# One mamba-and-attention decoder layer: two silus, the output projections and the keys and values in other slots of the scan

## What is computed

```python
x = x + mamba(layernorm(x))                        # the phase that the change touches
x = x + cross_attention(ctx, layernorm(x), mask)   # 750 keys per element, 16 heads
x = x + ffn(layernorm(x))                          # 2048 hidden, binarised weights, gelu
```

```python
xz = rmsnorm(h) @ W_in;  x, z = split(xz)          # 512 -> 2 x 1024
x = silu(conv4(x) + conv_b)
x_dbl = x @ W_x                                    # -> 64 for dt, 16 for B, 16 for C
dt = softplus(x_dbl[..., :64] @ W_dt + b_dt)
h[t] = exp(dt * A) * h[t-1] + (dt * x) * B         # 1024 x 16 states, over 224 steps
y = sum_n(h * C) + x * D
out = residual + (y * silu(z)) @ W_out
```

## Time and profile before

| | us |
|---|---|
| median of three runs | 3689.96 |
| the profiled execution | 3689.67 |
| its span, first to last instruction | 3688.3 |
| mamba phase: start of the first and of the last scan | 83.7 and 1983.8 |
| windows 1 to 13 together | 1563.2 |
| windows 14 and 15 | 114.2 and 103.3 |
| PE, DVE, ACT, POOL busy over the span | 3250.6, 2664.2, 2377.3, 1773.9 |

### The profile page before, as it was taken

One profiled execution on the slowest core, in us unless ns is written; L12 is line 12 of the kernel. 1 busy time (PEld: TensorE's weight loads), 2 busy tenths in 40 slices (PEclk: granted clock), 3 DMA queues, 4 the chain that ended last, 5 costly groups with the idle time before them and its releaser, 6 DMA issues. The chain is left out here.

```text
span 3688.3 us, 59573 instructions
## 1 busy us (share of the span) xinstructions
PE 3250.6 (88%) x20864; PEld 2278.9 (62%) x20864; DVE 2664.2 (72%) x4681; ACT 2377.3 (64%) x5276; POOL 1773.9 (48%) x1052
## 2 busy tenths in 40 slices
PE   5678888988898889898996799999999999789998
PEld 4556655666566656665563566666666666467887
DVE  2999999989898999889985566776766676422221
ACT  5877788677877787778863566766666666432222
POOL 2778787778877787878783000000000000035454
PEclk8799999999999999999998899999999999889999
DMA  6646756566657665666563231211211121111010
GB/s 172 185 121 178 192 164 159 158 185 181 164 139 199 182 158 153 181 188 160 143 183 101 74 90 45 82 51 45 74 58 45 50 82 46 30 54 46 23 46 23
DMA packets 286440, 425.14 MB, mean 115 GB/s; under 512 B 28641, under 2 KB 226273, under 8 KB 281538
## 3 DMA queue, kind: packets, MB, share of 16 engines
q1 hardware_dynamic: 273920, 410.75, 40.3%
q10 hardware_dynamic: 12226, 10.59, 1.0%
HBM read 320.25 MB, written 101.02 MB: 114 GB/s over the span
## 5 line engine op out<-in xcount | busy, mean ns | idle before, releaser
L704 POOL TENSOR_TENSOR a_hs<-a_rep,a_bmat 128x896 f32<-128x896 f32 x512 | 1060.2, 2092 | 327.2 <-PE a_yps L278 326.9
L603 DVE TENSOR_TENSOR_SCAN a_states<-a_states,a_hs 128x900 f32<-128x900 f32 x384 | 780.6, 2033 | 116.1 <-ACT a_states L384 111.7
L384 ACT ACTIVATE a_states<-a_rep,a_a_neg 128x224 f32<-128x224 f32 x2048 | 795.7, 438 | 69.3 <-DVE a_hs L610 66.9
L1208 DVE CUSTOM_DVE_ANT_0 b_sc<-b_sps,b_mask 112x375 f32<-112x375 f32 x1024 | 499.9, 544 | 148.3 <-PE b_sps L1019 148.0
L1035 PEld LDWEIGHTS b_tps<-b_ident,b_sc 112*125 112x125 f32 x3072 | 402.9, 191 | 279.3 <-issue 142.4
L1301 POOL TENSOR_TENSOR b_xt<-b_xt,b_bo 112x512 f32<-112x512 f32 x32 | 40.9, 1300 | 1067.9 <-DVE b_ln L1185 1067.9
L1035 PE MATMUL b_tps<-b_ident,b_sc 112*125 112x112 f32 x3072 | 492.9, 290 | 69.4 <-ACT b_sc L1126 45.3
L1126 ACT ACTIVATE b_sc<-b_sc,b_nmax 112x750 f32<-112x750 f32 x512 | 467.7, 915 | 51.9 <-DVE b_nmax L1214 51.9
L300 PE MATMUL a_work<-a_hT,w_in 128*128 128x224 f32 x2048 | 444.1, 374 | 52.4 <-ACT a_hT L416 46.1
L300 PEld LDWEIGHTS a_work<-a_hT,w_in 128*128 128x128 f32 x2048 | 410.8, 203 | 93.1 <-ACT a_hT L416 49.8
L610 DVE TENSOR_TENSOR a_hs<-a_states,a_cmat 128x896 f32<-128x896 f32 x384 | 419.0, 1091 | 13.2
(11 more groups left out here) (143 smaller groups left out, 4925.4 us busy)
## 6 DMA issues: line engine op xcount, KB each, us to landing
a_rep<-du_scratch SPq DMA_DIRECT2D x512, 224.0 KB, 5.7
w_in<-W_in_dram SPq DMA_DIRECT2D x128, 512.0 KB, 4.2
du_scratch<-a_du SPq DMA_DIRECT2D x16, 1792.0 KB, 10.9
ctx<-ctxT_dram SPq DMA_DIRECT2D x48, 500.0 KB, 5.2
v_scratch<-kv_out SPq DMA_DIRECT2D x96, 250.0 KB
k_scratch<-kv_out SPq DMA_DIRECT2D x96, 250.0 KB, 4.0
b_keys<-k_scratch SPq DMA_DIRECT2D x16, 1500.0 KB, 11.7
b_v<-v_scratch SPq DMA_DIRECT2D x16, 1500.0 KB
```

The source lines that it names most:

```text
L384: e = act.activation(rows(states[:, g % DA, :])[:, q, 1:ROW], rep[tile % REPS][:, j, 0, :], ACT.Exp, scale=a_neg[:, g % SLOTS, q:q + 1])
L603: dve.tensor_tensor_scan(state if g % G4 else whole, state, whole, 0.0, ALU.mult, ALU.add).then_inc(S["scan"], 1)
L704: pool.tensor_tensor(hs[g % RING][:, :, 1:ROW], rep[tile % REPS][:, j, 1, :].unsqueeze(1).broadcast_to([P, Q, L]), bmat[b % 2][:], ALU.mul ...
L1208: dve.tensor_tensor_reduce(out=sc[block % 2][:, j, cols], in0=sps[0:TT, j, 0:HALF], in1=mask[:, block % 2, cols], scale=-1.0, scalar=3.0e3 ...
```

## The change

Three edits to the tables, one to a condition. Both halves of the output projection move two slots later (11 and 14 become 13 and 16), and with them the residuals and the store of x1; the statistics of x1 stay in slot 20. In `LATER` the row statistics go from slot 3 to 4, the logs one slot earlier (9, 11, 13, 15), silu_z from 19 to 20. Silu_x stays. Of the keys and values units of a window the one in 13 goes to 11, that in 16 to 15, that in 20 to 18, and the one in 3 of the next window to 1 (in the element before the last, 13 to 11 and 16 to 15). The order of values and keys stays the same.

```diff
--- before.py
+++ after.py
@@ -125,7 +125,7 @@
     CHUNKS = t["ctxT"].shape[2] // KC
     WIDE = 2 * KC
     BEHIND = 4
-    O_SLOTS = (39 + BEHIND, 42 + BEHIND)
+    O_SLOTS = (41 + BEHIND, 44 + BEHIND)
     UNITS = 2 * CHUNKS
     OUTS = len(shared.kv_out)
     assert TT <= P and 2 * L <= BANK and R + 2 * N <= P and CHUNK <= 2 * BANK and R == 64 and DG == 32
@@ -212,12 +212,12 @@
             "series": spaced(14, 1), "logs": spaced(15, 1), "skip": [18, 19], "spread": [17], "dt_sum": [20],
             "silu_z": [21], "u": [21], "store_du": [22]}
         LATER = {
-            "load": [-68], "row_stats": [-65], "squares": [-60], "guess": [-58], "gains": [-54], "h": [-53], "hT": [-51],
+            "load": [-68], "row_stats": [-64], "squares": [-60], "guess": [-58], "gains": [-54], "h": [-53], "hT": [-51],
             "keep_hT": [-50], "load_x": spaced(-52, 4), "load_z": spaced(-50, 4), "x": spaced(-49, 4), "tap": spaced(-48, 4),
             "older_taps": spaced(-47, 4), "z": spaced(-47, 4), "keep_z": spaced(-46, 4), "residual": [-35], "silu_x": [-33],
             "x_dbl": [-32], "xd": [-31], "store_bc": [-31], "dt": spaced(-30, 2), "parts": spaced(-29, 2),
-            "series": spaced(-28, 2), "logs": spaced(-26, 2), "skip": [-20, -19], "spread": [-19], "dt_sum": [-18],
-            "silu_z": [-17], "u": [-16], "store_du": [-15]}
+            "series": spaced(-28, 2), "logs": spaced(-27, 2), "skip": [-20, -19], "spread": [-19], "dt_sum": [-18],
+            "silu_z": [-16], "u": [-16], "store_du": [-15]}
         when = [FIRST, SECOND] + [{name: [b * SLOTS + BEHIND + at for at in slots_of] for name, slots_of in LATER.items()}
                                   for b in range(2, B)]
 
@@ -225,8 +225,8 @@
 
             return [(b, i) for b in range(B) for i, at in enumerate(when[b].get(name, ())) if at == slot]
 
-        usual = (1, 3, 5, 9, 12, 16, 18, 20, 22, 24, 26, 31)
-        last_but_one = (1, 3, 5, 9, 12, 14, 15, 16, 18, 19, 20, 22, 23, 24, 26, 27, 28, 30)
+        usual = (1, 3, 5, 7, 11, 14, 18, 20, 22, 24, 26, 29)
+        last_but_one = (1, 3, 5, 7, 11, 14, 15, 16, 18, 19, 20, 22, 23, 24, 26, 27, 28, 30)
         last = (-1, 1, 2, 3, 5, 6, 8, 9, 12, 13, 14, 16, 17, 18, 20, 21, 22, 24)
         kv_slot = ([w * SLOTS + BEHIND + at for w in range(1, B - 2) for at in usual]
                    + [(B - 2) * SLOTS + BEHIND + at for at in last_but_one] + [(B - 1) * SLOTS + BEHIND + at for at in last])
@@ -665,7 +665,7 @@
                     at = slot - b * SLOTS
                     if at - 2 in O_SLOTS:
                         add_residual(b, O_SLOTS.index(at - 2))
-                    if at == O_SLOTS[1] + 6:
+                    if at == O_SLOTS[1] + 4:
                         x1_stats(b)
 
         def gpsimd_program():
```

## The result

| | us |
|---|---|
| before, median of 4 runs | 3689.68 |
| after, median of 4 runs (3724.31 to 3729.81) | 3728.48 |
| ratio, 95% interval | 1.0104 (1.0086 to 1.0121) |
| span of the profiled execution, before and after | 3688.3, 3728.3 |

The kernel became 1.0% slower where the prediction had it 2.0% faster, with 0.09 for slower. First the stretches of the changed kernel, in the columns of the earlier trace rows: window 0, windows 1 to 13, window 14, window 15, all behind the scan, and window 6 alone.

What follows compares the result with a forecast made beforehand. VectorE was held mainly by ScalarE's late decays, behind silus and copies of TensorE's results. Windows 120.2 to 114.8, times 13: -71; window 14 -4, window 15 +1: -74 on 3689.7 gives 3616 us, range 3598 to 3660.

Steps and rivals of the forecast that it cites:

- Slots 11 to 18: Keys, values and output projection moves there: projections end at 872.8, 0.4 us a window comes back (bounds 0 and 1.9).
- the residual, 0.4: Slot 18: VectorE's residual waits for the second output projection until 872.8, 0.4 us a window.
- the sum: Window: 109.55 busy, 1.2 between instructions, silu_x 1.2, silu_z 1.6, residual 0.4, plus 0.8: 114.8 us against 120.2.
- the 0.8 allowance: Added to each window because the chain has no slack: half of two costs bounded at 0.5 and 1.2 us.
- the prediction's own signs of being wrong: Slot 5 wait well under 1, none at slot 22, or TensorE gaps over 3 us between slots 18 and 33.
- one wait of 1.6 at scan 22: Slot 22: VectorE idle 1.6 us behind silu_z, where it was 2.24 at slot 21.
- The row statistics: Moved from slot 3 to 4: taken as 0 (bounds 0 and -1.2), the 1.2 us wait at scan 5 stays.
- The tap that silu_z stands behind: ScalarE, slots 19 to 22: the tap waits for x until 880.3, eating most of what the silu_z move promises.
- The waits at 25, 29 and 1: VectorE's waits at these slots, TensorE's pace: all go, -2.8 us a window.
- The decays of slot 13: Lengthened by the earlier log: end at 852.4 for a scan at 852.5, no loss (bounds 0 and +1.2 us).
- the last keys unit: Slot 35 to 33: its copy now precedes slot 4's decays; 0.7 us a window if TensorE were no earlier, taken as 0.
- (d): Rival, slower: low TensorE clock through a projection, 7 us more, 3712; turns where x of slot 19 ends over 5.3 later; 0.09.

Runs made afterwards that it cites:

- Experiments 9 and 10: The changed kernel with half of the second output projection left out, 3673.2 us; the changed kernel with three quarters of slot 18's keys unit left out, 3691.6 us.
- experiment 1: The changed kernel with skip copies in slots 18 and 19 instead of 16 and 17, product u and the store of dt and x one slot later: 3633.3 us.
- the silu part: Row statistics in slot 4 and silu_z in 20: alone on the kernel before, 3687.7 us (1.0000); undone on experiment 1, 3679.6 us.
- the better one: The kernel of experiment 1, the changed kernel with later skip copies: 3633.3 us.

## Why the prediction was wrong, step by step

**The step that failed** is "Slots 11 to 18". It followed the second projection to 872.8 on TensorE and then asked only who needs its result: the residual, 0.4. It didn't ask who waits for its input buffer to come free. ScalarE's skip copies of slots 16 and 17 do (`act.wait_ge(S["o_ps"], 2 * (b - 1))`), and the code of `skip` says so. The prediction's own times hold: it had the second projection end 26.4 behind the bank wait (872.8 less 846.4), and it ended 27.0 behind it (888.8 less 861.86). ScalarE was at the skip copy 19.0 behind it. In the kernel before the copy came 0.9 after the projection of slot 14, so its profile showed no wait there in any of windows 1 to 13. The term that was missing is the wait at scan 18, 96 us over these windows. Experiments 9 and 10 show that it goes with the projection's length and not with the work behind it.

The window came out at 122.9 where the sum had 114.8. The differences are 7.4 at scan 18, 2.1 at scans 21 and 22 (3.7 for 1.6) and 0.4 at scan 13, less the 0.4 for the residual, which didn't wait, the 0.8 allowance, and 0.75 by which VectorE was busy for less: 8.0 of the 8.1. One of the prediction's own signs of being wrong also came, a gap of TensorE of over 3 us between slots 18 and 33 (4.64).

That experiment 1 gained 95, so near to 96, is in part chance: its windows 1 to 13 are 89 us shorter than the change's, 6.9 each, and window 14 is 6.5 shorter.

**A smaller term** follows from it: the keys unit of slot 18 waits 4.64 for the residual at 895.51, and then takes 2.0 longer at TensorE's low clock (5.62 for 3.65). The prediction had one wait of 1.6 at scan 22; there are two, 1.54 at scan 21 and 2.14 at scan 22.

**What held.** The row statistics gave nothing: the wait at scan 5 is 1.20 in both kernels. The tap that silu_z stands behind is late, and most of that move is eaten. The waits at 25, 29 and 1 went, and the long ones at scan 23 too: windows 3 to 13 are all 122.9 long, where they were 119.1 to 122.0. The decays of slot 13 cost 0.4 (bounds 0 and 1.2). With the skip copies out of the way the windows are 116.1 long (1509.0 over 13) where the sum had 114.8, and the time 3633 where it had 3616. Two waits stand for most of it: 1.1 at scan 20, behind the copies in the tight stretch, and at scan 5 the 0.7 that the prediction had priced for the last keys unit and then put at 0. It is there in eight of the 13 windows (1.9 for 1.2), so that term was too low in a kernel that comes near the forecast.

**The rivals.** (d) put the slower side on this same stretch and nearly this price (3712), but by a low clock through a projection; the projections took 7.03 and 7.12, at full rate. Its point of turning was right (x of slot 19 later than 5.3): x ended 43.0 after that start (904.9 less 861.86) where 33.9 was forecast, 9.1 later, and the kernel was slower. The cause was another, so that this rival came so near in time is luck. The chance of 0.09 was too low because I had looked at each moved unit's results and never at who reuses its operands.

**Left open.** Window 0 is 2.8 longer, though nothing in it moved but one pair of row statistics. The eight kernels with the statistics in slot 4 have the same window 0, and it is 121.9 to 125.4 long; in the four with the statistics in 3 it is 121.3 to 123.0. So it seems to be the start's own variation; I didn't test it, and each length is that of one execution. Whether a third `yT` buffer, which needs 7,168 bytes more of each partition (8 tiles of 224 float32), removes the wait with the copies in place was not tried.

## What to carry to other kernels

When an instruction is moved later, list two sets of waiters: those who wait for its result, and those who wait to overwrite what it reads. The second set shows no wait in the profile as long as it is only just met, and it stands in the code as a wait on the reader's semaphore. On an engine with one queue the price isn't paid by the waiter but by what stands behind it, here the decays that pace the whole scan.

A move's worth also depends on its company: the silu part gave nothing on the kernel before and 46 us on the better one, so testing a move by itself can throw away a good one.

## What the runs showed of the hardware

TensorE was slower behind the time in which it stood for VectorE: after 4.64 us idle the keys unit took 5.61 to 5.87 instead of 3.65, in each of windows 1 to 13. The granted clock over that unit in window 6 was 0.64, so most of it ran at the lower level (1.2 GHz); over windows 1 to 13 it was 0.93 with the wait and 0.96 without it.

```profile
896.24:901.86 5.62, 5.62 (x17) 4.75 (x18) 5.58 (x5) 1.95 (x6) 5.62 (x3) 0.64 0.30 93
```
The Trainium skill ("TensorE: Matmul & The Clock Gate", Part 1: The HAM clock gate) has idle time lowering the clock, and the rows agree. The prediction feared a fall behind the new short gaps ahead of the partial sums; behind a gap of 1.95 before the sums of slot 24 in the changed kernel they took 1.73, no longer than without one.
